# Softmax attention: value products of three key tiles in one group, four exponential buffers, a new table of places, and up products between the last steps

## What is computed

```
x = x + tanh(g_xattn[0]) * L0_xattn(layernorm(x), ctx)     # linear attention, 16 heads of 8
x = x + tanh(g_ffn[0])   * L0_ffn(layernorm(x))            # quantised gate/up/down, inner 512
x = x + tanh(g_xattn[1]) * L1_xattn(layernorm(x), ctx)     # softmax attention
x = x + tanh(g_ffn[1])   * L1_ffn(layernorm(x))            # 8 experts, the best 2 of each row

# L1_xattn
scores  = qh @ kh.T / sqrt(8);  attn = softmax(scores)     # 16 heads, 56 queries, 1500 keys
context = attn @ vh;            return context @ W_o.T + b_o
# L1_ffn: gelu(x @ w1[e] + b1[e]) @ w2[e] + b2[e], summed over the two experts by their weight
```

## Time and profile before

| | us |
|---|---|
| median of the runs (760.61, 760.64, 759.10) | 760.61 |
| profiled execution, its own time | 760.72 |
| its span, first to last instruction | 758.9 |
| windows 0 to 15 of the softmax attention | 238.0 to about 641.4 |
| an even window in the middle (b = 6) | 395.26 to 421.37, 26.11 |
| an odd window in the middle (b = 7) | 421.37 to 447.97, 26.60 |
| window 12, 13, 14 | 23.77, 24.96, 23.13 |
| last `weigh` to first `up` of the experts | 641.4 to 651.6 |

### The profile page before, as it was taken

One profiled execution on the slowest core, in us unless ns is written; L12 is line 12 of the kernel. 1 busy time (PEld: TensorE's weight loads), 2 busy tenths in 40 slices (PEclk: granted clock), 3 DMA queues, 4 the chain that ended last, 5 costly groups with the idle time before them and its releaser, 6 DMA issues.

```text
span 758.9 us, 19249 instructions
## 1 busy us (share of the span) xinstructions
PE 668.7 (88%) x7270; PEld 467.6 (62%) x7283; DVE 538.9 (71%) x1252; ACT 507.5 (67%) x807; POOL 270.8 (36%) x324
## 2 busy tenths in 40 slices
PE   3599999997267999999999999999999988899997
PEld 3477777775133666666655666666566665577777
DVE  5799999998968887888878878878877761212122
ACT  4487777775524778877787787788788866533441
POOL 4298888884341232234214313312333010000000
PEclk9899999999758999999999999999999999799999
DMA  4122222252460663665376356636654580201110
GB/s 142 40 82 82 81 81 81 81 158 53 37 140 32 137 155 98 133 133 135 88 165 133 99 116 132 145 93 152 132 124 113 112 185 5 65 29 53 33 42 25
DMA packets 59379, 74.42 MB, mean 98 GB/s; under 512 B 35320, under 2 KB 40178, under 8 KB 59306
## 3 DMA queue, kind: packets, MB, share of 16 engines
q1 hardware_dynamic: 59306, 73.39, 40.9%
HBM read 32.35 MB, written 1.40 MB: 44 GB/s over the span
## 4 chain that ended last, share of the span: by engine, by line
PE 43%; DVE 15%; issue 7%; POOL 2%; ACT 2%; SPq 1%; another core or an unknown queue 1%; DMA 1%; DVEq 0%; POOLq 0%; ACTq 0%
DVE mx L1586 8%; PE ps L654 8%; PE ps L741 7%; PE ps L802 7%; PE ps L814 7%; PE ps L728 6%; PE ps L640 4%; PE ps L646 2%; DVE kvall L1417 2%; PE ps L676 1%; DVE amax L1456 1%; POOL KP L1103 1%; DVE silu L1501 1%; ACT P L992 1%
## 5 line engine op out<-in xcount | busy, mean ns | idle before, releaser
L992 ACT ACTIVATE P<-ps,kbias,kscale 125x896 f32<-125x896 f32 x192 | 210.3, 1097 | 86.7 <-PE ps L728 83.6
L1586 DVE TENSOR_REDUCE mx<-ps 128x1 f32<-128x500 f32 x336 | 214.2, 671 | 47.2 <-PE ps L654 45.4
L654 PE MATMUL ps<-KP,Qb 128*128 128x500 bf16 x336 | 129.7, 388 | 15.9 <-DVE mx L1586 9.8
L1103 POOL TENSOR_TENSOR KP<-kvall,KP 128x1500 bf16<-128x1500 f32 x16 | 48.6, 3039 | 231.4 <-ACT KP L935 231.4
L741 PE MATMUL ps<-P,Vp 125*32 125x112 f32 x3072 | 114.5, 267 | 2.3 <-ACT P L992 1.2
L741 PEld LDWEIGHTS ps<-P,Vp 125*32 125x32 f32 x3072 | 68.0, 110 | 52.7 <-issue 38.2
L531 PE MATMUL ps<-wkv,cT 128*125 128x256 f32 x384 | 92.7, 385 | 0.5 <-ACT arena L892 0.5
L531 PEld LDWEIGHTS ps<-wkv,cT 128*125 128x125 f32 x384 | 70.1, 192 | 9.7 <-issue 0.9
L892 ACT ACTIVATE arena<-ps,arena 125x128 f32<-125x128 f32 x192 | 54.8, 368 | 27.5 <-DVE arena L1291 13.9
L1053 ACT ACTIVATE arena<-ps,b 128x448 f32<-128x448 f32 x64 | 40.4, 633 | 47.5 <-PE ps L802 41.7
L728 PE MATMUL ps<-QS,KS 128*128 128x112 bf16 x768 | 68.9, 215 | 2.4 <-DVE QS L1592 1.4
(11 more groups left out here) (213 smaller groups left out, 1015.6 us busy)
## 6 DMA issues: line engine op xcount, KB each, us to landing
cT<-ctxT_dram SPq DMA_DIRECT2D x32, 750.0 KB, 4.1
KS<-KP SPq DMA_DIRECT2D x48, 375.0 KB, 7.2
arena<-KP SPq DMA_DIRECT2D x48, 375.0 KB, 7.3
QS<-QD SPq DMA_DIRECT2D x96, 28.0 KB, 5.6
wgu<-w_dram SPq DMA_DIRECT2D x8, 256.0 KB, 3.0
silu<-w_dram SPq DMA_DIRECT2D x8, 256.0 KB, 2.9
x<-xh_dram SPq DMA_DIRECT2D x1, 512.0 KB, 3.5
mixed<-att SPq DMA_DIRECT2D x16, 28.0 KB
```

The lines of the kernel that those rows point to most:

```text
L654: ins = nc.tensor.matmul(ps[:, bank, 0:KCW], q[:, 128 * c:128 * c + 128], KP[par][0][:, KCW * k:KCW * k + KCW], start=True, stop=True)
L992: nc.scalar.activation(P[t % 2][0:TK, :].rearrange("p (k n) -> p k n", k=2), src, ACT.Exp, scale=kscale[0:TK, bass.ds(n, 1)], bias=kbias[0 ...
L1103: nc.gpsimd.tensor_tensor(KP[par][2][:], krest, KP[par][1][:], ALU.subtract).then_inc(sem("kp3_ready"), 1)
L1586: ins = v.tensor_reduce(mx[:, c, k:k + 1], ps[:, bank, 0:KCW], AX.X, ALU.max)
```

## The change

`P` has four buffers in place of two; the two new ones lie in `arena`, from column 6016. The exponential of tile t goes to `P[t % 4]` and waits for `weigh` of tile t - 4 where it waited for that of t - 2. TensorE no longer weighs a tile behind each tile's scores, but three tiles in a row behind the scores of tiles 3, 6 and 9, and the last three behind the first scores of the next window. The last window (b = 15) keeps the old order (`apart`). The table has new places: in even windows V0 moves from tile 4 to 1, AT from 1 to 2, OT from 2 to 3 ahead of the group, DE behind it, K0 from 5 to 4, V1 from 6 to 5, K2 from 9 to 8, XT from 8 to 9; in odd windows V1 moves from tile 3 to 2, OT from 2 to 3, K2 from 9 to 8, ET from 8 to 9. At the end, `up` runs over halves first, so that its first four products need only the first eight sequences; two of them stand around `OT`, two behind `FO`, and the logits of tiles 0 to 6 stand behind `FT` and behind the two ups; the last logits stand behind `ET`. The logits are in bank 4.

```
 PLACES = [
-    [[["MX0"], ["Q1"], ["MX1"]], [["MX2"], [], ["AT", "MX3"]], [["MX4"], ["OT"], ["MX5"]],
+    [[["MX0"], ["Q1"], ["MX1"]], [["MX2"], ["V0"], ["MX3"]], [["MX4"], ["AT"], ["MX5"]],
...
+TOGETHER = 3
...
-        P = [sb(f"P{n}", [128, HQ]) for n in range(2)]
+        P = [sb(f"P{n}", [128, HQ])[:] for n in range(2)]
+        P += [arena[:, PAT + HQ * n:PAT + HQ * n + HQ] for n in range(2)]
...
+                apart = fixed(i) and w == B - 1
                 for t in range(T):
                     scores(at, t, 0, first)
                     units_at(t, 0)
                     scores(at, t, 1, first)
                     units_at(t, 1)
-                    if t > 0:
+                    if t == 0:
+                        if not first:
+                            for before in range(T - TOGETHER, T):
+                                weigh(w - 1, 1 - par, before, first_pair)
+                    elif apart:
                         weigh(w, par, t - 1, first_pair)
-                    elif not first:
-                        weigh(w - 1, 1 - par, T - 1, first_pair)
+                    elif t % TOGETHER == 0:
+                        for before in range(t - TOGETHER, t):
+                            weigh(w, par, before, first_pair)
                     units_at(t, 2)
...
+            pe.wait_ge(sem("side_free"), emptied((NT - 1, 1), "ET"))
+            up(0, 0, True, range(0, 1))
             fill(AFTER, "OT", B - 1, 1)
-            for unit in LAST:
-                fill(AFTER, unit, NT - 1, 1)
+            up(0, 0, True, range(1, 2))
+            fill(AFTER, "FT", NT - 1, 1)
+            logits(range(0, 3))
+            fill(AFTER, "FO", NT - 1, 1)
+            up(0, 0, True, range(2, 4))
+            logits(range(3, NT - 1))
+            fill(AFTER, "ET", NT - 1, 1)
...
             def exponentials(b, par, t, first):
...
-                if not (first and t < 2):
-                    act.wait_ge(sem("pv_done"), n - 1)
+                if not (first and t < 4):
+                    act.wait_ge(sem("pv_done"), n - 3)
...
             def inner(e, par, first_pair):
...
-                    c, k = divmod(u, 2)
+                    k, c = divmod(u, FC)
```

41 lines of the change are left out of this document (23 added, 18 removed), and 14 rows, old and new, of the table PLACES.

## The result

| | before | after |
|---|---|---|
| median of the runs, us | 760.61 | 780.50 (779.8 to 781.93) |
| profiled execution, its own time | 760.72 | 781.93 |
| its span | 758.9 | 780.1 |
| an even window in the middle (b = 6) | 26.11 | 28.36 |
| an odd window in the middle (b = 7) | 26.60 | 27.78 |

The changed kernel is 2.7% slower: ratio 1.0269, 95% interval 1.0249 to 1.0289. The prediction was 769.5 us with a range of 739 to 776. The direction was right; the size was not, 8.9 us against 19.9, and 780.5 lies above the range. The experiments were timed in five later series, each beside its own runs of the kernel before, whose medians were 759.3 to 760.1; small differences between series go by the ratios.

The account below looks back on a forecast made before the run. TensorE was taken as the bound in the middle windows, with VectorE and ScalarE near. Windows +13.5 us and the end -4 on 760.7 gave 770.2, rounded to 769.5 us, range 739 to 776.

Parts of the forecast that it names:

- "-0.5 together" for windows 0 and 1: Windows 0 and 1, without Q1, FO or ET: 0.5 us less together, between -3.8 and 1.5.
- "0" for window 12: Window 12, Q1 but no chain, little VectorE work: -1.9 + 1.2 + 0.7 for side units, no change.
- "-1.8" for window 13: Window 13, where VectorE has 17.75 us of work in 24.96: 1.8 us less.
- the end: Behind the last `weigh`: ups and logits moved into the waits save 4 us, between 1.5 and 5.5.
- towards the old time: Final rounding of the sum from 770.2 to 769.5 us, because small gaps the walk keeps can close.
- TensorE busy under 23.5: Sign to look for in the changed trace: TensorE busy under 23.5 us in each window.
- the walk: Step through even window 6, adding waits one after another: it ends at 28.1 us, 2.0 more than before.
- the two waits: Even windows: TensorE stands 1.2 us at V0 for VectorE's reading of Q1, another 1.2 at OT for AT's copy.
- I take 0.9: Odd windows: 0.9 us more each, between 1.9 less and 2.0 more.
- Rival 1: Whole kernel: TensorE's saving arrives, 2.9 us less for a pair of windows, 738 us; chance 0.24.
- Rival 3: Even windows: the two 1.2 us waits lower the clock, 8.5 us more, 778 us; chance 0.06.
- rival 2: Whole kernel: gain and loss cancel, -3.5 with 2 either way, given as 757 to 762 us; chance 0.14.

Follow-up runs that it names:

- e1: The changed kernel with the old table of places; groups of three, four buffers and the new end stay: 775.99 us, ratio 1.0223.
- e9: Groups of three, old table, Q1 read early, plus VectorE's two quantising steps one MX later in odd windows: 771.87 us, ratio 1.0166.
- e13: Groups of three, old table, Q1 early, quantising one MX later, plus GpSimd's last_deviation ahead of its third key part: 763.50 us, ratio 1.0045.
- e14: The changed kernel with Q1 read early and GpSimd's last_deviation ahead of the key part: 772.91 us, ratio 1.0179.
- e16: The kernel before with the new end and last_deviation ahead of the key part; no groups, old table: 755.68 us, ratio 0.9946.
- e17: Groups of three, old table, Q1 early, quantising one MX later, last_deviation first, plus maxima over 250 of 500 columns: 753.17 us, ratio 0.9906.
- e5: Groups of three with the old table and the new end, and VectorE reading Q1 ahead of MX1: 771.71 us, ratio 1.0160.
- e8: Groups of three with the old table and the new end, each maximum over 250 of 500 columns: 760.34 us, ratio 1.0007.
- e4: The changed kernel with VectorE reading Q1 in its own turn, ahead of MX1 and not behind MX2: 775.39 us, ratio 1.0210.

## Why the prediction was right in direction and short in size

**The step that failed.** It is three terms of the sum: "-0.5 together" for windows 0 and 1, "0" for window 12 and "-1.8" for window 13. They were priced on the premise that TensorE's saving arrives where VectorE has little work or no Q1, FO or ET. Together they stood at -2.3 us and measured +5.5, which is 7.9 of the 11.8 us between forecast and result (21.3 in the profiles against 13.5 - 4). What the runs showed in its place are waits for single instructions, which little work does not remove, and in window 0 a stretch at the lower clock besides. The ten full windows account for 2.2 us of the miss, the end for 1.3, window 14 for 0.4. Rounding 770.2 "towards the old time" took the number another 0.7 the wrong way.

**TensorE's side was right.** 1.28 us for a group (measured 1.29). Counted from start to start, all that stood 0.15 us or more above the shortest such step in the trace comes to 1.6 and 1.4 us in windows 6 and 7 before, and to 4.9 and 4.7 after. So the rest of TensorE's time fell from 24.5 and 25.2 us to 23.4 and 23.0, by 1.1 and 2.1; the forecast was 1.9. The sign "TensorE busy under 23.5" was wrong: the view counts 24.65, since the modelled end of a matmul ahead of a stand covers part of the stand (V0 stood 1.17 from the pace, and its row shows 1.01).

**Even windows were right in size, and in the waits named:** 28.36 against 28.1, with V0, OT and DE within 0.12 us of the walk. Part of this is luck. The walk runs along the delay of the groups, yet the table alone makes the same window (28.40), with other waits: V0 1.0, OT only 0.2, reductions 1.6. The walk's own rows give V0's wait without any group, Q1 read out at 3.5 (398.78 - 395.26) and V0 reached at 1.52 + 0.83 = 2.35: it is V0's new place behind Q1, whose reading is late by its own place on VectorE. And the two waits explain 1.6 to 2.0 of 2.25 us, not all.

**Odd windows were nearly right for a wrong reason:** +1.18 against +0.9, "I take 0.9" being a sum of small gaps on VectorE. On the old table e1, e9 and e13 show one chain over three engines instead: cast on ScalarE, GpSimd's key part, Qb and QD, `rstd`, `xe` on VectorE, reductions, MX; it is worth 0.83 us there. In the changed kernel the same move gave back only 0.24 of the 1.18 (27.77 to 27.53, e14), and the new table alone makes 0.7 of an odd window. What makes the rest is not traced to one cause. The prediction followed the cast to the stacked keys, and GpSimd's queue only that far; it didn't ask what else stands in that queue.

**The other windows** carry most of the miss:
- Window 13: +1.1 against -1.8. It was priced as a window in which the saving arrives, since VectorE has little to do there. But TensorE stood 0.88 us ahead of OT, for ScalarE's copy of V1, and 0.97 ahead of an MX, where before one stand of 0.8 for an MX was the longest; e14 halves the second by moving the deviation. On the old table e13 brought this window to 24.49, 0.5 below before; but that is still above the 24.08 of the same move without groups (e16).
- Window 12: +1.9 against 0. The walk had the saving (1.9), V0's wait (1.2) and 0.7 for the other side units. Counted as above, TensorE stood 3.4 us: 1.2 ahead of V0, 1.0 for reductions, 0.4 for ScalarE's reading of K units, 0.3 for the maxima ahead of SH and 0.5 for the stacked keys, where before it stood nowhere for 0.15 us. That is 1.5 more than the walk had, and TensorE's saving there is 1.5 and not 1.9.
- Windows 0 and 1: +2.6 against -0.5. Nearly all is window 0, its row below, with a mean clock of 0.86 where it was 0.91 before. TensorE stood 2.6 us for reductions, and right behind the longest of these stands, 1.1 us, the clock went to its lower level for 3.4 us, the second row.

```profile
237.95:266.90 28.95, 25.65 (x304) 17.13 (x306) 22.17 (x48) 19.42 (x24) 7.56 (x9) 0.86 0.43 87
256.40:259.80 3.40, 3.40 (x13) 1.66 (x13) 2.16 (x7) 1.82 (x3) 0.00 (x0) 0.50 1.06 206
```

The same window took 25.74 with the group on the old table, 31.47 with the table alone and 26.78 in e14 in their profiles, so its part isn't steady, and I leave its cause open beyond this.
- Window 14: +1.7 against +1.3, behind the keys as forecast:

```profile
648.60 0.69 PE L731 MATMUL ps<-QS,arena 128*128 128x112 bf16 x8 [3.04 <-DMA QS<-QD]
```

**The end** gave 2.7 us where 4 were forecast, in the profiles; this term of the sum was mis-sized. From the last `weigh` (640.90 before, 665.67 after) to the first step behind the ups (665.87 and 687.08) it is 24.97 and 21.41, so 3.56 sooner; but window 15 up to its last `weigh` is 0.9 longer (16.19 and 17.07), since three products of window 14 stand in it, and the sum had 0 for window 15. Up 5 started 10.7 us behind the last `weigh`, as forecast (651.5 - 640.9 = 10.6), but the twelve ups took 10.7 us and not 9.0, the first 3.4 of them at the lower clock. The order of events was as described: logits, exponential, table load, gelu, ups, with the lower clock for another stretch:

```profile
673.15 0.39 PE L807 MATMUL ps<-gw_sb,xT 128*128 128x8 f32 x2 [0.45 <-ACT xT L1031]
676.35 10.89 PE L801 MATMUL ps<-xT,wgu 128*128 128x448 f32 x24 [2.81 <-ACT arena L1074]
...
676.20:679.60 3.40, 3.25 (x5) 1.61 (x6) 2.62 (x12) 2.31 (x5) 0.00 (x0) 0.50 0.34 102
...
674.37 1.28 ACT L1074 ACT_TABLE_LOAD   x1
```

**The rivals.** Rival 1, the saving arrives, had 0.24: no kernel here came near it, not even e17, in which Q1, the quantising steps and the deviation are mended and 4 us of VectorE's work are gone. Rival 3 was near in time (778) and wrong in mechanism: all windows from 1 to 14 kept 1.00, window 6 with its two stands of about 1.1 us. Its price was right where the clock did fall. In the profile of e14 one even window (b = 8) took 29.00 and not 27.44, with the same stands and a clock of 0.94:

```profile
398.57:426.02 27.45, 24.33 (x364) 16.96 (x365) 20.75 (x52) 20.33 (x29) 8.78 (x12) 1.00 0.55 120
453.55:482.55 29.00, 25.77 (x363) 18.25 (x364) 20.84 (x52) 20.32 (x29) 8.77 (x12) 0.94 0.50 114
```

The clock fell at 461.8, 0.5 us behind the end of OT's stand of 1.34 us, and stayed down for 3.4 us. In the profiles of e1, e5 and e8 it fell in window 13, 1.0 to 1.6 us behind the end of a stand of 2.1 to 2.3 us. The rule that idleness lowers the clock (the Trainium skill, "TensorE: Matmul & The Clock Gate") agrees with these places. But the stand of 1.34 us in the other even windows of e14, and the 2.3 us in window 13 of e9, left the clock at 1.00, and no run here shows what decides.

**Two sums of the prediction** are off without changing the forecast. The last transfers of window 6 land at 414.27 + 5.6 - 395.26 = 24.6 us after its start, not at "24 at most". And rival 2's own sum, -3.5 with 2 either way, gives 755 to 759, not 757 to 762.

## What to carry to other kernels

Grouping a short operation shortens its own engine's work and keeps that engine from serving the others for as long as the group lasts; count what the other engines need from it in that time, and try the smallest group first. When an instruction moves by half a microsecond, follow every queue that it feeds to the end, the small instructions behind the large ones too: two tiny GpSimd instructions behind 6 us of others were worth 8.4 us on the old table (e13 against e9). In the changed kernel they were worth 2.5 (e14), half of what Q1's place was (5.1, e4), so what a wait is worth holds for one order of the queues only. Windows with little work are not the ones where a saving arrives of itself; there, a wait in a queue stands uncovered.
